# Q and K parts copied inside SBUF, the opening reordered, and TensorE fed the mask while it waits

## The reference

```python
Q = (layernorm(x) @ Wq.T); K = (c @ Wk.T); V = (c @ Wv.T)      # split in 16 heads of 16
scores = where(causal, Q K^T, -inf) / sqrt(16)
x = x + tanh(g_xattn) * (softmax(scores) V @ Wo.T + bo)
```

```python
logits = layernorm(x) @ controller + tie                       # per group of 32 tokens
perm = (logits == max over the group)
x = x + tanh(g_ffn) * combine(perm, relu(dispatch(perm, layernorm(x)) f1 + bias) f2)
```

## Time and profile before

| | us |
|---|---|
| median of 3 runs | 309.49 (307.36 to 311.57) |
| the profiled execution | 311.98 |
| its span in the profile | 310.3 |
| PE, DVE, ACT, POOL busy | 243.7, 197.7, 168.3, 124.1 |

### The profile page before, as it was taken

How to read it: one execution, slowest core, us unless ns; L and a number is a source line. 1 busy time by engine, 2 the same in 40 slices (tenths; PEclk the granted TensorE clock), 3 DMA queues, 4 the chain that set the end, 5 groups by cost and what they waited for, 6 DMA issues and landing times.

```text
span 310.3 us, 8572 instructions
## 1 busy us (share of the span) xinstructions
PE 243.7 (79%) x3426; PEld 193.9 (62%) x3426; DVE 197.7 (64%) x433; ACT 168.3 (54%) x345; POOL 124.1 (40%) x230
## 2 busy tenths in 40 slices
PE   0617163798989899898888878698998888789995
PEld 0617052776768687686666656476766777677773
DVE  4574755496859779485777799989995443412222
ACT  1521243485877768485757645336785443334553
POOL 4140233557776767675556665624541000000000
PEclk9985765599999999799989999979999999859999
DMA  6929985647677675738551000049940000001211
GB/s 175 212 92 185 288 167 100 142 109 163 149 178 139 150 162 133 162 65 182 116 138 23 4 4 5 0 145 396 388 161 2 3 4 4 4 2 68 69 68 68
DMA packets 21961, 35.87 MB, mean 116 GB/s; under 512 B 2915, under 2 KB 15779, under 8 KB 20387
## 3 DMA queue, kind: packets, MB, share of 16 engines
q1 hardware_dynamic: 21059, 34.01, 43.1%
q10 hardware_dynamic: 864, 1.33, 1.9%
HBM read 26.65 MB, written 8.39 MB: 113 GB/s over the span
## 4 chain that ended last, share of the span: by engine, by line
PE 27%; POOL 24%; issue 23%; DVE 13%; DMA 7%; ACT 4%; SPq 1%; POOLq 0%; DVEq 0%
POOL pT L377 9%; PE banks L763 7%; PE banks L735 6%; DMA cT<-in_ctxT_dram 6%; PE banks L472 4%; PE banks L772 3%; POOL xs L371 3%; POOL qp L362 3%; POOL kp L362 2%; DVE permb L1144 2%; POOL onl L401 2%; DVE rsum L1099 2%; DVE gmax L1130 1%; PE banks L581 1%; DVE lt L1125 1%
## 5 line engine op out<-in xcount | busy, mean ns | idle before, releaser
L1091 DVE TENSOR_REDUCE nmax<-banks 128x4 f32<-128x512 f32 x64 | 43.7, 685 | 37.5 <-PE banks L535 37.5
L377 POOL TENSOR_SCALAR_AFFINE_SELECT pT<-pT 128x512 f32<-128x512 f32 x64 | 40.7, 637 | 45.4 <-ACT pT L866 45.3
L866 ACT ACTIVATE pT<-banks 128x512 f32<-128x512 f32 x64 | 37.6, 590 | 8.2 <-PE banks L552 7.8
L871 ACT ACTIVATE banks<-cb 128x512 f32<-128x512 bf16 x62 | 37.0, 596 | 5.6 <-DVE nmax L1091 5.5
L581 PE MATMUL banks<-pT,va 128*32 128x128 f32 x512 | 27.7, 289 | 0.8 <-POOL pT L377 0.8
L535 PE MATMUL banks<-kst,qst 96*128 96x128 bf16 x256 | 26.7, 231 | 1.7 <-ACT banks L871 1.4
L1099 DVE RECIPROCAL rsum<-banks 128x256 f32<-128x256 f32 x16 | 28.0, 1748 | 0.0
L552 PE MATMUL banks<-qst,kst 99*128 99x128 bf16 x256 | 25.9, 225 | 1.0 <-ACT pT L866 1.0
L581 PE MATMUL banks<-pT,ones 128*32 128x128 f32 x512 | 26.4, 279 | 0.0
L763 PEld LDWEIGHTS banks<-cf,routed 128*128 128x128 f32 x128 | 21.1, 250 | 7.2 <-issue 6.2
L985 ACT ACTIVATE ys<-banks 128x1024 f32<-128x1024 f32 x16 | 16.7, 1046 | 16.0 <-PE banks L763 16.0
(11 more groups left out here) (115 smaller groups left out, 633.4 us busy)
## 6 DMA issues: line engine op xcount, KB each, us to landing
wx<-in_wexp_dram SPq DMA_DIRECT2D x32, 256.5 KB, 6.8
q_rows<-qp SPq DMA_DIRECT2D x8, 384.0 KB, 2.5
k_rows<-kp SPq DMA_DIRECT2D x8, 384.0 KB, 4.9
qst<-q_rows SPq DMA_DIRECT2D x8, 384.0 KB, 4.7
kst<-k_rows SPq DMA_DIRECT2D x8, 384.0 KB, 4.8
cT<-in_ctxT_dram SPq DMA_DIRECT2D x8, 256.0 KB, 6.7
qst<-q_rows SPq DMA_DIRECT2D x8, 256.0 KB, 5.5
kst<-k_rows SPq DMA_DIRECT2D x8, 256.0 KB, 5.6
```

The source lines that it names most:

```text
L377: pool.affine_select(p, p, [[0, HC], [1, P]], ALU.is_ge, 0.0, base=0, channel_multiplier=-1)\
L866: act.activation(pT[:, n % PR, :], BT[n % 2], ACT.Exp, scale=float(D) ** -0.5).then_inc(p_ready, 1)
L871: act.activation(BS[n % 2], causal, ACT.Copy).then_inc(mask_placed, 1)
L1091: dve.tensor_reduce(nmax[:, b % 2, :].rearrange("p (e j o) -> p e o j", e=2, o=KH)[:, e, o], BS[n % 2].rearrange("p (j t) -> p j t", j=HC) ...
```

## The change

In groups, as the diff has it:

- **Copies.** `keep_rows` and the two DRAM tensors go. Each of the six stripes of a stack becomes one transfer from `kp` or `qp` in SBUF to the stack in SBUF (128 KB, 128 pieces of 1 KB), issued by SP as soon as its part is ready: high three times, mid twice, low once. `high_part` of the next group now waits until the whole stack of the group before has landed. Issued in the loop are the low part of Q for the next group, then high, mid and low of K, then `place_max` and the context, then high and mid of Q.
- **Loads.** Only the identity (64 KB) of the constants is loaded at the start, by ACT, with the K and Q weights. V's weights and the gates move to SP behind `x` and context; WO's, the other constants and the controller come last in the opening; the last 8 entries of `x` come in two loads. The ones rows of `kst` come later, context 1 earlier.
- **Opening on the engines.** POOL makes the mask first and takes the low part of K's weights (in four pieces); DVE makes the first low part of Q; K of group 1 is projected before `x` of group 1 is turned; the statistics of entries 2 to 7 are taken at once, in front of `k_rest(0)`, and their 13 steps are spread between the splits. `weight_high(WO)` and `weight_low(WO)` move into slots 11 and 12, the controller's copy into slot 56.
- **Mask products.** `keep_warm(16)` on PE: 16 products of the mask with itself (128 x 128 by 128 x 512, bf16) before the first turn of `x`, and 16 more between `project_q(1)` and the loop.

```diff
-XL = ((0, 2), (2, 4), (4, 8), (8, 16))
+XL = ((0, 2), (2, 4), (4, 8), (8, 12), (12, 16))
+COPIES = 6 * 16
...
+            def stack(st, at, g, parts, i, ready, stacked):
+                sp.wait_ge(ready, g + 1)
+                sp.dma_start(st[at * D:(at + 1) * D, g % STACKS].rearrange("p h b c -> p (h b c)"), parts[:, i, :])\
+                    .then_inc(stacked[g % STACKS], 16)
+            def stack_free(g):
                 if g >= STACKS:
                     sp.wait_ge(t_done, 2 * NC * (g - STACKS + 1))
...
+            def stack_k_high(g):
+                stack_free(g)
+                for at in (2, 4, 5):
+                    stack(kst, at, g, kp, 2, kh_ready, k_stacked)
+            def stack_k_mid(g):
+                for at in (1, 3):
+                    stack(kst, at, g, kp, 1, km_ready, k_stacked)
+            def stack_k_low(g):
+                stack(kst, 0, g, kp, 0, kl_ready, k_stacked)
...
             load_x(0)
             load_context(0)
+            sp.wait_ge(x_loaded[0], 16)
+            load_context(1)
+            load_x(1)
+            load_x(2)
+            sp.dma_start(w[:, V], wattn[:, V]).then_inc(w_loaded[V], 16)
+            sp.dma_start(gb[:, :], gbo).then_inc(gates_loaded, 16)
             sp.wait_ge(shift_ready, 1)
             sp.dma_start(kst[SROWS:TROWS]...).then_inc(shift_stacked, 16)
-            load_x(1)
-            load_context(1)
-            load_x(2)
-            keep_q(0)
-            keep_k(0)
-            stack_q(0)
-            stack_k(0)
+            load_context(2)
+            stack_k_high(0)
+            stack_k_mid(0)
+            stack_k_low(0)
+            stack_q_high(0)
+            stack_q_mid(0)
+            stack_q_low(0)
             load_x(3)
-            load_context(2)
-            keep_q(1)
-            keep_k(1)
-            stack_q(1)
-            stack_k(1)
+            stack_k_high(1)
+            stack_k_mid(1)
+            stack_k_low(1)
             load_context(3)
+            stack_q_high(1)
+            stack_q_mid(1)
+            load_x(4)
+            sp.dma_start(w[:, WO], wattn[:, WO]).then_inc(w_loaded[WO], 16)
+            sp.dma_start(cf[:, P:], constf[:, P:]).then_inc(consts_loaded, 16)
             sp.dma_start(ctrl_in[:, :, :], ctrl).then_inc(small_loaded, 16)
             for g in range(NG2 + 1):
                 if g >= 1:
                     place_max(2 * g - 1)
-                if 1 <= g < NG2 - 1:
-                    keep_q(g + 1)
-                    stack_q(g + 1)
+                if g + 1 < NG2:
+                    stack_q_low(g + 1)
                 if g + 2 < NG2:
-                    keep_k(g + 2)
+                    stack_k_high(g + 2)
+                    stack_k_mid(g + 2)
+                    stack_k_low(g + 2)
                 if g < NG2:
                     place_max(2 * g)
-                if g + 2 < NG2:
-                    stack_k(g + 2)
                 if g + 4 < NG2:
                     load_context(g + 4)
+                if g + 2 < NG2:
+                    stack_q_high(g + 2)
+                    stack_q_mid(g + 2)
...
             # POOL, opening
+            weight_low_by_dim(K)
             context_low(0)
-            low_part(qp, 2, qr, 1, 0, qm_ready, ql_ready)
+            context_low(1)
             low_part(kp, 0, kr, 1, 0, km_ready, kl_ready)
-            context_low(1)
-            low_part(qp, 2, qr, 1, 1, qm_ready, ql_ready)
             low_part(kp, 0, kr, 1, 1, km_ready, kl_ready)
+            weight_low(V)
             context_low(2)
-            weight_low(V)
-            pool.wait_ge(small_loaded, 16)
-            pool.tensor_copy(ctrl_sb...).then_inc(ctrl_ready, 1)
-            weight_low(WO)
...
             # PE, opening
-            pe.wait_ge(consts_loaded, 16)
+            def keep_warm(times):
+                for _ in range(times):
+                    pe.matmul(bank[1], causal[:, 0:P], causal, start=True, stop=True)
+            pe.wait_ge(masks_ready, 2)
+            keep_warm(16)
+            pe.wait_ge(ident_loaded, 16)
             transpose_x(0, BB)
...
+            for o in range(KH):
+                project_k(1, o, bank[5])
             transpose_x(1, bank[3])
-            for o in range(KH):
-                project_k(1, o, bank[5])
             for o in range(KH):
                 project_q(1, o, bank[2])
+            keep_warm(16)
...
             # ACT
+            def high_part(parts, i, of, g, done, stacked, ready):
                 act.wait_ge(done, g + 1)
                 if g >= 1:
-                    act.wait_ge(kept, 16 * g)
+                    act.wait_ge(stacked[(g - 1) % STACKS], COPIES * ((g - 1) // STACKS + 1))
                 act.activation(parts[:, i, :], of, ACT.Copy).then_inc(ready, 1)
...
+            weight_high(K)
             context_high(0)
-            weight_high(K)
             weight_high(Q)
+            context_high(1)
             xT_high(0, BB)
             k_high(0)
+            k_mid(0)
             q_high(0, bank[4])
             q_mid(0)
-            k_mid(0)
-            context_high(1)
+            k_high(1, bank[5])
+            k_mid(1)
             xT_high(1, bank[3])
-            k_high(1, bank[5])
+            weight_high(V)
+            context_high(2)
             q_high(1, bank[2])
             q_mid(1)
...
             # DVE, opening
             normalize_x(1)
-            weight_low(K)
             weight_low(Q)
+            statistics(2, 4, 2)
             xT_low(0, BB)
+            statistics(4, 8, 2)
+            stages(2, 8, 0, 4)
             k_rest(0)
+            stages(2, 8, 4, 8)
             q_rest(0, bank[4])
-            rstd_rows(2, 4)
+            stages(2, 8, 8, 10)
+            q_low_first()
+            stages(2, 8, 10, RSTD_STAGES)
+            rstd_ready(2)
             normalize_x(2)
             normalize_x(3)
+            k_rest(1, bank[5])
             xT_low(1, bank[3])
-            k_rest(1, bank[5])
             q_rest(1, bank[2])
-            rstd_rows(4, 8)
```

More of the change, by code:

```diff
@@ L366, in weight_low, with weight_low_by_dim @@
                 pool.tensor_tensor(wl[:, m], w[:, m], wh[:, m].bitcast(F32), ALU.subtract).then_inc(w_low[m], 1)
+            def weight_low_by_dim(m):
+                pool.wait_ge(w_high, 1)
+                for j in range(2 * KH):
+                    out, high = [t[:, m].rearrange("p k (o d h) -> p (k o) d h", o=KH, d=D)[:, j] for t in (wl, wh)]
+                    last = pool.tensor_tensor(out, w[:, m].rearrange("p k (o h d) -> p (k o) d h", o=KH, d=D)[:, j],
+                                              high.bitcast(F32), ALU.subtract)
+                last.then_inc(w_low[m], 1)
             def bias_x(b):
@@ L435, in _ @@
                     split_out(n // 4 - 4)
[L436 removed]
+                if s == 1 and g + 1 < NG2:
                     low_part(qp, 2, qr, 1, g + 1, qm_ready, ql_ready)
@@ L439, in _ @@
                     low_part(kp, 0, kr, 1, g + 2, km_ready, kl_ready)
+                if n == 12:
+                    weight_low(WO)
                 if s % 4 == 2 and n // 4 < NB:
@@ L787, in _ @@
         def _(act):
-            act.dma_start(cf[:, :], constf).then_inc(consts_loaded, 16)
-            for i in range(2):
+            act.dma_start(ident, constf[:, 0:P]).then_inc(ident_loaded, 16)
+            for i in (K, Q):
                 act.dma_start(w[:, i], wattn[:, i]).then_inc(w_loaded[i], 16)
@@ L793, in _ @@
             act.activation(warm[:, :], warm[:, :], ACT.Exp)
-            for i in range(2, 4):
-                act.dma_start(w[:, i], wattn[:, i]).then_inc(w_loaded[i], 16)
-            act.dma_start(gb[:, :], gbo).then_inc(gates_loaded, 16)
             def context_high(g):
@@ L933, in _ @@
                     k_mid(g + 2)
+                if n == 11:
+                    weight_high(WO)
                 if s == 4 and g + 3 < NG2:
@@ L991, in _, with step @@
             steps = [0]
-            def step(ins):
+            chain = {}
+            def step(ins, lo):
                 steps[0] += 1
+                chain[lo] = steps[0]
                 ins.then_inc(dve_step, 1)
@@ L1000, in rstd @@
                 m, q, v, y, t = mv[:, lo:hi, 0], mv[:, lo:hi, 1], ve[:, lo:hi], rs[:, lo:hi], nt[:, lo:hi]
-                if stage > 0:
-                    dve.wait_ge(dve_step, steps[0])
+                if stage > 0 or lo in chain:
+                    dve.wait_ge(dve_step, chain[lo])
                 if stage == 0:
@@ L1034, in statistics @@
                     last = dve.bn_stats(stats[:, b, :], xs[:, b, :])
-                step(last)
+                step(last, of)
             dve.memset(warm[:, :], 0.0).then_inc(act_warm, 1)
             dve.memset(shift[:, :], 1.0).then_inc(shift_ready, 1)
-            def rstd_rows(lo, hi):
-                statistics(lo, hi)
-                rstd_ready()
-                for stage in range(RSTD_STAGES):
-                    rstd(stage, lo, hi)
-                rstd_ready()
             def normalize(b, ready):
```

(29 more changed lines are left out.)

109 lines of the change are left out of this document (46 added, 63 removed).

## The result

The changed kernel took 315.83 us (median of 4 runs, 313.26 to 319.13) against 310.53 before: a ratio of 1.020 (95% interval 1.012 to 1.028): not faster, and whether it is slower by 2% is not decided. Beside later runs it took 314.52 against 310.97, 1.008 (0.991 to 1.026). Ratios and intervals leave out slow executions (over 1.5% above the fastest of the same kernel), so they differ a little from the quotients of the medians, which are of all executions. I had forecast 293.3 and 286.5 to 302.

A forecast was written before the change was run, and what follows sets the result against it. PE was busy 243.7 of 310.3 us, so its waits in the opening were the target: slot 8 17.5 us earlier, less 1.3 in the loop, gives 16.2; from a median of 309.49 to 293.3 us, range 286.5 to 302.

The forecast's parts named there:

- The stripe's price: Opening copies: a stripe into 16 partitions takes 0.7 us, so group 0 is stacked at 24.4 us, against 34.3 before.
- My upper bound, 0.87: Stripe copies: at most 0.87 us each, a third of the 384 KB DRAM write that took 2.6 us.
- Who waits for a stripe: Opening, group 1: `k_high(1)` waits for group 0's K stack until about 20.3 us; Q then starts on PE at 23.5.
- the sum would be the same: Opening: even at 1.2 us a stripe, group 0 is stacked at 28 us, before PE is ready, so the total stays.
- `k_rest(0)`: Opening, behind the statistics of `x` entries 4 to 7: runs from 15.0 to 15.8 us; before it ended at 15.7.
- The mask products: Opening on PE: first 16 cost nothing; second 16 run from 26.0 to 30.9 us, bounds 29.4 and 32.9.
- rival 2: Slots 0 to 7: PE's clock falls again, 1.8 us or more a slot; gain 8 to 12, 299.5 us; chance 0.15.
- the 248.9 us after it: Everything after slot 8's old start at 61.42 us: keeps its work and is carried over.
- WO's splits: Slots 11 and 12: `weight_high(WO)` and `weight_low(WO)` cost 1.3 us there, bounds 0 and 1.9.
- my 16.2: Whole kernel: total gain in us, slot 8 coming 17.5 earlier less 1.3 in the loop.
- Rival 5: Loop's DMA queue: it becomes the bound if stripes cost over 1.4 us; at 1.9, 329 us; chance 0.06.
- rival 4: Opening's order: late `x` entries 4 to 7 and queued stripes eat the gain, under 6, 305 us; chance 0.07.

The follow-up runs named there:

- e3: The kernel before with only its copies changed, to SBUF to SBUF stripes into 16 neighbouring partitions: 335.51 us, ratio 1.077.
- e12: The changed kernel (neighbouring stripes) with its late loads, 1 MB, issued behind the first row maximum: 313.93 us, ratio 1.012.
- e14: The changed kernel with stripes six partitions apart and its late loads, 1 MB, issued behind the first row maximum: 302.85 us, ratio 0.969.
- e15: The changed kernel (neighbouring stripes) without any mask products: 309.45 us, ratio 0.999.
- e10: The changed kernel with stripes six partitions apart and without any mask products: 295.60 us, ratio 0.946.
- e1: The changed kernel (neighbouring stripes) without the second 16 mask products, those in front of the loop: 317.50 us, ratio 1.026.
- e8: The changed kernel with stripes six partitions apart and without the second 16 mask products: 302.19 us, ratio 0.972.
- e7: The changed kernel with each stripe put into 16 partitions six apart instead of 16 neighbours: 298.07 us, ratio 0.953.
- e9: The kernel before with only its copies changed, to SBUF to SBUF stripes into 16 partitions six apart: 304.25 us, ratio 0.979.

## Why the prediction was wrong, step by step

- **The stripe's price** is the step that failed first: "Nearest is the old third stripe ... it took 0.6 us more. I take 0.7." Measured alone 1.36 us. The row gave landing times of three transfers that were in flight together, the first two into 48 and 32 partitions; the difference of two landings is not the third one's cost. The same rows give for all three, 768 KB, 6.6 us from the first issue to the last landing (0.84 and 5.8), 118 GB/s by my estimate and not 210. The same reading made me keep the rule of the Trainium skill out of the sum. My upper bound, 0.87, was too low as well; it came from a write out of 128 partitions to DRAM, which has no 16 target partitions. An issue takes SP 0.60 us, where I had 0.42. Six apart, the price is at most 0.66 and slot 8 comes at 44.9, where the forecast had 43.9 and neighbours give 58.2. Part of that closeness is luck: the first scores came 1.8 us later than forecast (32.7, not 30.9) and slots 0 to 7 took 0.8 less (12.2, not 13.0).
- **Who waits for a stripe.** I let `k_high(1)` wait to 20.3; it was 24.2, and 21.45 with stripes six apart. So "the sum would be the same", said of a stripe at 1.2 us, was wrong too: I had put that price on group 0's last landing alone, and not on this wait. I did not follow the same wait to group 2 (40.1 and 52.4), where the late loads and their stripes stand in one queue, nor the maximum behind 1 MB ("behind it there is less than before" was said of the loop alone). These waits took the place of the 5.0, 9.9 and 5.6 us that did go.
- **`k_rest(0)`** behind the early statistics: forecast to start at 15.0, it did at 16.0. Right in kind, 1 us early.
- **The mask products** on the path: forecast 30.9 for their end, from a start at 26.0; they ran from 30.27 to 34.95, 4.8 us as forecast, later only because the stack was. The clock was not full from 29 to slot 8, as I had it, but at half again from 39.6 to 49.7 us and from 53.3 on, with PE busy 7.14 of 10.1 us in the first of these: the fall of rival 2, at 0.15, came beside the waits. With stripes six apart it was full from 30.6 on but for 40.8 to 44.1. I said that the first set costs nothing. In the opening that is so. The 6 to 8 us that either set alone costs, most of it in the experts' stage, lay in no row that I could have read, but I carried over "the 248.9 us after it" as unchanged, and PE's instructions ahead of them had changed.
- **WO's splits**: 1.3 us forecast; no cost shows, and the scatter of 2 us and more hides one of this size.
- **The account.** Without products and with stripes six apart the change gives 295.60, 14.5 us under the 310.13 beside it; my 16.2 was near that, but for another kernel, as it counted the mask products in. Neighbouring stripes take 13.9 of it (309.45 to 295.60, both without products), the products another 5 to 6 in the medians (309.45 to 314.52 and 315.83), though one of eight executions of the changed kernel took 309.72.

Rival 5 named the DMA queue; its point of decision, 1.4 us a stripe, was nearly met at 1.36, and e3 shows it happening. At 0.06 it was priced too low, because the row against it had been misread. But it is not what the changed kernel shows: its loop was hardly longer. That kernel lost its gain in the opening's queue, where rival 4 came nearest (gain under 6; 3.2 came, though not by late entries of `x`), and in the experts' stage, which no rival had.

## What to carry to other kernels

A transfer that regroups many partitions into few should spread its target rows over the partitions: any order of rows will do for a product that sums over them, and here a step of six instead of one was worth 11 to 18 us in the kernels that differ only in it (e12 to e14, e15 to e10, e1 to e8, changed to e7), and 31 us where stripes come in a bunch (e3 to e9). The cost of one transfer is not the difference between the landings of transfers in flight together; measure a run of them alone. And instructions added early in TensorE's stream can cost in a far stage, as here where its clock then fell earlier: time a kernel with and without them before crediting them with anything.

## What was not expected of the hardware

- Twelve transfers of 128 KB into 16 neighbouring partitions took 17.8 us from SBUF and 16.1 from DRAM; six apart 9.4; into 128 partitions 9.1.
- In the experts' stage PE was busy for 40.8 of 44.2 us at a mean clock of 0.62, and the clock did not come back while it ran: products of 32 rows or 32 columns with 64 columns to move. Before its fall (237.1 to 247.8 us) PE was busy 84% of the time, after it (247.8 to 281.3) 95%.
- Sixteen near-empty products (0.60 us of PE's time) at the start made a kernel of 295.60 us take 302.56.
- The way from 32 more instructions to the earlier fall of the clock stays open, and so does whether another number would push the fall past the stage's end, as in one profile of the changed kernel (+34.4 us, stage 34.8).
